# Ternary down product as two passes over divided rows, and the small inverse roots as a power on GpSimd

## The reference

```python
xn = layernorm(x)
x = x + L0_attn(xn) + L0_ffn(xn)        # layer 0
xn = layernorm(x)
x = x + L1_attn(xn) + L1_ffn(xn)        # layer 1: rotary attention; attention block and a top-2 mixture of 8 experts

def L0_ffn(x):                          # ternary weights, hidden width 1024
    gate, up = split(x @ ternary(w_gate_up).T)
    h = silu(gate) * up
    hn = h * rsqrt(mean(h * h) + eps)   # one factor per token, applied after the product in the kernel
    return hn @ ternary(w_proj).T       # the "down product"

def L0_attn(x):
    xn = rmsnorm(x)
    # q, k, v, gate, decay; a scan over time per (head, value) with a state S; group norm over 16 heads; silu gate; @ Wo
    x = x + gated @ Wo
    return x + swiglu(rmsnorm(x) * ln2) @ W2         # hidden width 704
```

## Time and profile before

| | |
|---|---|
| median of three runs | 671.49 us (668.30 to 672.75) |
| the profiled execution's own time | 671.92 us |
| its span in the trace | 670.1 us |
| mean granted TensorE clock | 0.938 of full |
| busy: PE, PE weight load | 570.6, 410.1 us |
| busy: DVE, ACT, POOL | 476.0, 309.0, 219.7 us |

### The profile page before, as it was taken

One profiled execution on the slowest core, in us unless ns is written; L12 is line 12 of the kernel. 1 busy time (PEld: TensorE's weight loads), 2 busy tenths in 40 slices (PEclk: granted clock), 3 DMA queues, 4 the chain that ended last, 5 costly groups with the idle time before them and its releaser, 6 DMA issues.

```text
span 670.1 us, 10996 instructions
## 1 busy us (share of the span) xinstructions
PE 570.6 (85%) x3694; PEld 410.1 (61%) x3694; DVE 476.0 (71%) x1054; ACT 309.0 (46%) x569; POOL 219.7 (33%) x226
## 2 busy tenths in 40 slices
PE   1777799889588999998999888988888799999990
PEld 1543467668367788883455545454444588888870
DVE  5789966797775477759787787778862477777753
ACT  2748322313322333551665635545537556666630
POOL 2667556546553533673200010010044012111210
PEclk9989889989698999995899999999989899999995
DMA  5221600000220000278353121200044891000005
GB/s 183 83 90 53 238 0 1 1 0 14 77 80 16 1 1 22 95 235 277 92 167 97 50 80 34 64 2 2 3 156 179 329 384 58 32 24 25 24 32 196
DMA packets 27404, 58.61 MB, mean 87 GB/s; under 512 B 4262, under 2 KB 19142, under 8 KB 24742
## 3 DMA queue, kind: packets, MB, share of 16 engines
q1 hardware_dynamic: 25094, 52.59, 24.2%
q0 software_dynamic: 1872, 5.13, 2.2%
q10 hardware_dynamic: 384, 0.20, 0.1%
HBM read 45.14 MB, written 15.51 MB: 90 GB/s over the span
## 4 chain that ended last, share of the span: by engine, by line
PE 40%; DVE 11%; ACT 3%; POOL 2%; issue 2%; DMA 1%; SPq 0%; ACTq 0%; POOLq 0%; DVEq 0%
PE bank L833 19%; DVE small L1826 5%; PE bank L1096 5%; PE bank L1073 4%; PE bank L827 4%; PE bank L1046 4%; PE bank L1048 1%; PE bank L1075 1%; ACT PTa L1381 1%; DMA yt<-results 1%; PE bank L1113 1%; POOL P3c L2254 1%; POOL rt L2194 1%; DVE XA L1855 1%; POOL P L2254 1%
## 5 line engine op out<-in xcount | busy, mean ns | idle before, releaser
L1826 DVE TENSOR_REDUCE small<-bank 128x1 f32<-128x256 f32 (+3 forms) x256 | 107.5, 483 | 7.5 <-PE bank L1048 6.6
L1046 PE MATMUL bank<-Ks,Qs 96*128 96x256 bf16 (+3 forms) x256 | 66.8, 328 | 8.7 <-DVE small L1826 7.1
L2088 DVE TENSOR_TENSOR wl<-wall,wh 128x1024 fp32r<-128x1024 f32 x46 | 56.2, 1222 | 22.0 <-ACT wh L1527 20.7
L1073 PE MATMUL bank<-Qs,Ks 99*128 99x512 bf16 (+3 forms) x256 | 59.4, 308 | 1.6 <-ACT PTa L1381 1.2
L1381 ACT ACTIVATE PTa<-bank 128x512 f32<-128x512 f32 (+1 forms) x96 | 43.5, 530 | 33.7 <-PE bank L1075 31.4
L1381 ACT ACTIVATE PTb<-bank 128x512 f32<-128x512 f32 (+1 forms) x96 | 43.8, 530 | 27.9 <-PE bank L1075 27.4
L1048 PE MATMUL bank<-maskb,identb 128*128 128x128 bf16 x256 | 55.4, 234 | 0.0
L1073 PEld LDWEIGHTS bank<-Qs,Ks 99*128 99x128 bf16 x256 | 25.5, 99 | 44.0 <-issue 24.0
L1330 ACT ACTIVATE sg<-bank 128x512 f32<-128x512 f32 (+1 forms) x28 | 16.7, 598 | 69.9 <-PE bank L833 69.9
L1527 ACT CAST wh<-wall 128x1024 fp32r x46 | 48.0, 1044 | 1.7 <-issue 0.5
L1075 PE MATMUL bank<-identb,maskb 128*128 128x128 bf16 x256 | 47.5, 223 | 0.0
(11 more groups left out here) (356 smaller groups left out, 1529.5 us busy)
## 6 DMA issues: line engine op xcount, KB each, us to landing
wall<-e_pack SPq DMA_DIRECT2D x8, 1536.0 KB, 8.7
Ks<-pieces SPq DMA_DIRECT2D x48, 128.0 KB, 2.6
Qs<-pieces SPq DMA_DIRECT2D x48, 128.0 KB, 2.7
stg<-w_pack SPq DMA_DIRECT2D x18, 256.0 KB, 2.8
pieces<-P SPq DMA_DIRECT2D x9, 512.0 KB, 5.1
wf<-t_pack SPq DMA_DIRECT2D x12, 256.0 KB, 2.7
sorted_rows<-blank_pack SPq DMA_DIRECT2D x1, 2967.0 KB, 14.3
yt<-results SPq DMA_DIRECT2D x8, 256.0 KB, 4.7
```

What stands on the lines that cost most here:

```text
L1046: nc.tensor.matmul(banks[b][:, o:o + w], Q[0:96, h, i * P:(i + 1) * P], K[0:96, h, 0:w], start=True, stop=False)
L1073: nc.tensor.matmul(banks[b][:, o:o + w], K[0:99, h, j * P:(j + 1) * P], Q[0:99, h, j * P:CH], start=True, stop=False)
L1826: last = nc.vector.tensor_reduce(mxv[:, i, h:h + 1], banks[b][:, o:o + w], AX.X, ALU.max, negate=True)
L2088: nc.vector.tensor_tensor(weight_part("l", i, half), wall[:, bass.ds(place + half * KC * EI, KC * EI)], weight_part("h", i, half).bitcast( ...
```

## The change

1. Down product. ACT casts hm to fh (fp32r), DVE makes fl = hm - fh (fp32r), and PE multiplies both with wpr as fp32r, two single passes in place of one fp32 product. `out` now waits for fl of its step. The item ("fl", s) is in the slot of `in`, one late on DVE, with no rank, so it stands behind the scan of that slot. On ACT the cast stands in front of the square.
2. Roots. All roots of 4 and 8 columns past the first norm are made by one POOL instruction, `inverse_roots`: small[:, 1] = small[:, 0] to the power -0.5, which waits for the DVE instruction that makes v (`variances_ready`); the users of the root wait for `inverse_roots`. A column of -0.5 is set at the start.
3. Order. In slots under 35 the DVE items that make v of `ss` and of ("rms", 0) come first in their slot; the users ("ssx", and ("rms", c, 1)) come last in theirs. The first norm (slots before 0) and the 64-column roots are as before.

```diff
+        m7, _ = plan([("fixed", [CH], F32), ("fh", [2, CH], F32R), ("fl", [2, CH], F32R)], o)
...
-            put(FF_SLOT[s], ("in", s), ("hm", s))
+            put(FF_SLOT[s], ("in", s), ("hm", s), ("fl", s))
...
-        put(22, ("ss", 0))
-        put(34, ("ss", 1))
+        put(22, ("ss", 0), ("ssx", 0))
+        put(34, ("ss", 1), ("ssx", 1))
...
+                if engine == "DVE" and slot < SW_AT and (op == "ss" or it == ("rms", 0, 0)):
+                    op = "first"
...
             def mlp_out(s, yb):
-                pe.wait_ge(*(hmr if kind == "ff" else alr).upto(s))
+                pe.wait_ge(*(flr if kind == "ff" else alr).upto(s))
...
-                        terms = [(hm[:, r, t * P:(t + 1) * P], L0["wpr"][:, m, :].bitcast(F32))]
+                        terms = [(part[:, s % 2, t * P:(t + 1) * P], L0["wpr"][:, m, :]) for part in (L0["fh"], L0["fl"])]
...
             def mlp_high(s):
+                    if s >= 2:
+                        act.wait_ge(*y.upto(s - 2))
+                    else:
+                        act.wait_ge(*t_put.upto(PIECES[-1]))
+                    nc.scalar.copy(L0["fh"][:, s % 2, :], hm[:, s % 3, :]).then_inc(*fhr.tick(s))
...
+            def mlp_low(s):
+                dve.wait_ge(*fhr.upto(s))
+                if s >= 2:
+                    dve.wait_ge(*y.upto(s - 2))
+                nc.vector.tensor_tensor(L0["fl"][:, s % 2, :], hm[:, s % 3, :], L0["fh"][:, s % 2, :].bitcast(F32), ALU.subtract)\
+                    .then_inc(*flr.tick(s))
...
+            def ff_squares(c):
+                dve.wait_ge(*mm.upto(("ss", c)))
+                nc.vector.tensor_scalar(small[:, 0, 0:TPC], banks[3][:, 0:TPC], 1.0 / 1024, EPS_F32, ALU.mult, ALU.add)\
+                    .then_inc(*var.tick(("ff", c)))
+                dve.wait_ge(*var.upto(("ff", c)))
...
             def ff_out(c):
-                rsqrt(r, v, TPC, 4)
+                dve.wait_ge(*inv.upto(("ff", c)))
...
-                    elif it[2] in (1, 2):
-                        rms_factors(it[2])
-                    else:
+                    elif it[2] == 1:
+                        rms_squares(("xm", c))
+                    elif it[2] == 3:
                         ln2_rows(c)
...
+            def inverse_roots(key, n):
+                pool.wait_ge(*var.upto(key))
+                nc.gpsimd.tensor_tensor(small[:, 1, 0:n], small[:, 0, 0:n], minus_half.broadcast_to([P, n]), ALU.pow).then_inc(*inv.tick(key))
...
+                elif op == "ss":
+                    inverse_roots(("ff", it[1]), TPC)
+                elif op == "rms" and it[2] == 0:
+                    inverse_roots(("rms", it[1]), TPC)
+                elif op == "xm" and it[2] == 1:
+                    inverse_roots(("xm", it[1]), TPC)
+                elif op == "ln" and it[2] == 0:
+                    inverse_roots(("norm", it[1]), 2 * TPC)
```

More of the change, by code:

```diff
@@ L170, in build @@
         ah_at = mlp_at + (2 + 3) * CH * 4
+        minus_half = small[:, 11, 63:64]
         QSX = at("QSX", [6, CH], F32, ah_at)
@@ L521, in build @@
         put(29, ("wo", 0, 1))
-        put(32, ("rms", 0, 0))
+        put(32, ("rms", 0, 0), ("rms", 0, 1))
         put(33, ("xat", 0, 0), ("xat", 0, 1))
@@ L541, in build @@
         put(SW_AT + SWO_AT[2], ("l1", 0, "xt", 0), ("l1", 0, "xt", 1))
-        LATE = {"PE": {}, "ACT": {"hm": 1}, "POOL": {"hm": 1, "read": 1},
-                "DVE": {"upd": 1, "scan": 1, "tern": 1, "hm": 1, "tr": 1, "proj": 1, "otok": 1, "wo": 1, "ss": 1, "got": 1, "xat": 1}}
+        LATE = {"PE": {}, "ACT": {"hm": 1}, "POOL": {"hm": 1, "read": 1, "ss": 1},
+                "DVE": {"upd": 1, "scan": 1, "tern": 1, "hm": 1, "fl": 1, "tr": 1, "proj": 1, "otok": 1, "wo": 1, "ss": 1, "ssx": 1, "got": 1, "xat": 1}}
         RANK = {"PE": ("rep", "in", "tern", "red", "out"), "ACT": ("in", "hm", "ternA"),
-                "POOL": ("read", "tern", "hm"), "DVE": ("tern0", "hm", "upd", "tern", "scan")}
+                "POOL": ("read", "tern", "hm"), "DVE": ("first", "tern0", "hm", "upd", "tern", "scan")}
         def order_of(engine):
@@ L1600, in norm_stats, with norm_squares @@
                     dve.wait_ge(*factors.upto(c))
+            def norm_squares(c):
+                v = small[:, 0, 0:2 * TPC]
+                stats(X, c)
+                tell(nc.vector.tensor_scalar(v[:, 0:TPC], mv[:, :, 1], EPS, None, ALU.add))
+                nc.vector.tensor_scalar(v[:, TPC:2 * TPC], mv[:, :, 1], 1.0 + EPS, EPS * EPS, ALU.mult, ALU.add)\
+                    .then_inc(*var.tick(("norm", c)))
             def norm_rows(layer, c):
+                if layer == 1:
+                    dve.wait_ge(*inv.upto(("norm", c)))
                 r1, r2 = small[:, 1, 0:TPC], small[:, 1, TPC:2 * TPC]
@@ L1732, in group_norm, with rms_squares @@
                     nc.vector.tensor_tensor(nat(L0["cen"]), nat(L0["cen"]), wide(rs_), ALU.mult).then_inc(*tok.tick(("got", c)))
[L1734 to L1741, removed]
-                else:
-                    newton(r, v, TPC, 4, 2)
+            def rms_squares(key):
+                v = small[:, 0, 0:TPC]
+                link(nc.vector.tensor_tensor(v, mv[:, :, 0], mv[:, :, 0], ALU.mult))
+                nc.vector.scalar_tensor_tensor(v, v, EPS, mv[:, :, 1], ALU.add, ALU.add).then_inc(*var.tick(key))
+                dve.wait_ge(*var.upto(key))
             def rms_scale(c, dst, key):
                 r = small[:, 1, 0:TPC]
+                dve.wait_ge(*inv.upto(("rms", c)))
                 for t in range(TPC):
@@ L1756, in ln2_rows @@
                 dve.wait_ge(s_route, 16)
+                dve.wait_ge(*inv.upto(("xm", c)))
                 for t in range(TPC):
@@ L2004, in _ @@
                 elif op == "rms":
-                    for pr in range(2):
-                        dve.wait_ge(*dproj.upto(("wo", it[1], pr)))
-                    rms_rows(it[1], L0["cen"], "xat")
+                    c = it[1]
+                    if it[2] == 0:
+                        for pr in range(2):
+                            dve.wait_ge(*dproj.upto(("wo", c, pr)))
+                        stats(XA, c)
+                        rms_squares(("rms", c))
+                    else:
+                        rms_scale(c, L0["cen"], "xat")
                 elif op == "swout":
@@ L2010, in _ @@
                 elif op == "ln":
-                    (norm_stats if it[2] == 0 else norm_rows)(1, it[1])
+                    norm_squares(it[1]) if it[2] == 0 else norm_rows(1, it[1])
                 elif op == "l1":
```

27 lines of the change are left out of this document (14 added, 13 removed).

## The result

Over 20 runs the changed kernel takes 666.47 us in the median (663.44 to 672.61), the kernel before 670.39 (667.87 to 673.29). The ratio is 0.9942, with a 95% interval of 0.9923 to 0.9962: 0.6% faster. The forecast was 666.9 with a range of 661.0 to 672.0.

A forecast was written before the change was run, and what follows sets the result against it. PE was taken to bound the feed-forward slots, DVE's chain the xm attention. Terms +0.2, 0, -0.5 and -4.3 gave -4.6: the span of 670.1 becomes 665.5, the time forecast 666.9 us, range 661.0 to 672.0.

The forecast's parts named there:

- What fl costs: Feed-forward slots: fl adds 0.60 us on DVE to hm, upd and scan, 3.05 us a slot together.
- The port makes it 3.2: Steady feed-forward slots: read, acc and fl take turns at the shared SBUF port, so a slot takes 3.2 us.
- fl(0) and hm(1): First feed-forward step: fl(0) waits behind a read until 92.1, so hm(1) moves from 90.27 to 92.0, 1.7 us late.
- The reduction of the group norm 2.2 earlier: Feed-forward slots: the group norm's reduction on DVE starts 2.2 us earlier than before.
- v to power 6 us, X rows 132.6, down product 134.4, DVE idle 2 to 3 in front of fl(10), hm(11) 144.0: End of the first batch: power's wait about 6 us, X rows and down product 1.8 earlier, hm(11) 1.8 later.
- Then PE's shorter products win back half: hm(15) is 1.4 late.: Last feed-forward slots: of hm(12)'s 3 us delay, PE's shorter products recover half, leaving hm(15) 1.4 us late.
- the second rival: Feed-forward slots: fl waits for fh in every slot, DVE's slot is 3.4 to 3.6 us, time 670.5; chance 0.12.
- POOL's queue takes another 0.5: End of the slots: POOL's queue of reads and low parts loses another 0.5 us to fl(15), ending at 176.7.
- The power's price 0.5, upper end 1.3: Each power instruction on POOL, on 4 or 8 columns: taken as 0.5 us, bounds 0.2 to 1.3.
- First power 5.5 us slow: Rival: only the first power, at the first batch's stall, is slow by about 5.5 us, time 672.4; chance 0.07.
- rms of the second batch 0, last norm -0.5: Second batch: no change at the rms before its cen, and the second layer norm's rows 0.5 us earlier.
- xm -4.3: Layer 1's attention, two xm norms: DVE's root leaves the chain, 2.15 us gained each, -4.3 for both.

The follow-up runs named there:

- fh_first: Changed kernel with ACT's order within a slot turned round, so fh and the square precede the next step's sg; 662.32 us, ratio 0.9868.
- both_moves: Changed kernel with fh ahead of sg on ACT, first batch's power ahead of read and sum, first rms' power ahead of the last low part; 659.55 us, ratio 0.9848.
- down_only: Kernel before with the down product's part alone (fh, fl, two fp32r passes), small roots still Newton rounds on DVE; 668.46 us, ratio 0.9994.
- xm_only: Kernel before with nothing changed but the power in the two xm norms; 665.46 us, ratio 0.9921.
- roots_only: Changed kernel with the old fp32 down product straight from hm; powers and their order stay; 666.34 us, ratio 0.9936.
- power_ahead: Changed kernel with only POOL reordered: first batch's power ahead of read and sum, first rms' power ahead of the last low part; 663.19 us, ratio 0.9889.
- power_twice: Changed kernel with every power done twice, one behind the other; 671.73 us, ratio 1.0010.
- short_acc: Changed kernel with POOL's sum of squares over 8 of 512 columns in all but a batch's first step; 667.07 us, one run.
- fp32_ahead: Changed kernel with the powers early on POOL, the old fp32 down product and ACT's order unchanged; 661.25 us, ratio 0.9861.
- lows_later: both_moves with five of the six low parts of w1 and w3 behind POOL's last reads and the first rms' power; 663.19 us, ratio 0.9870.

## Why the prediction was right, and where it was not

The mechanism in the attention was right. The total was right by compensation, and in part by luck: the terms below, with their measured sizes, add up to only 1.7 of the 3.9 us that were measured. 0.67 us of the +2.96 in the table had come before the first hm; 2.3 belong to the stage. By the steps of the prediction:

- *"What fl costs": DVE 3.05 us a slot.* Right, measured 3.04, with PE's sum just as long. *The port makes it 3.2*: wrong in steady slots. DVE's fl was in time and POOL's read paid, 1.66 instead of 1.29 us, which POOL had to spare. The wait itself is there: fl(6) starts at 112.43 beside a read that ends at 113.02 and lasts 1.14. The Trainium skill ("GPSIMD Engine Reference", 1. Specifications) says that such instructions contend; the trace agrees, 1.66 and 1.14 against 1.29 and 0.67. The rule was right, and yet it was no bound here.
- *fl(0) and hm(1).* hm(1) was forecast at 92.0 and came at 92.56, with the stage 0.67 late. But the reason was another: fl(0) had 1.14 us of idle time for ACT's cast, not for the read.
- *The reduction of the group norm 2.2 earlier.* It started at 119.79; before, at 122.24. Counted from the first hm that is 3.1 us earlier, 0.9 more than I had.
- *v to power 6 us, X rows 132.6, down product 134.4, DVE idle 2 to 3 in front of fl(10), hm(11) 144.0.* Measured 6.7, 133.20, 135.01, 2.73 and 144.56. Less the 0.67 us by which the stage began late, the three times hold within 0.2 us; from v to the end of the power it is 0.7 more than I had. It is luck that the times fit so well: the port's 0.16 us a slot did not come, and waits for fh at fl(0), fl(2), fl(6) and fl(7) that I hadn't counted there took their place.
- *"Then PE's shorter products win back half: hm(15) is 1.4 late."* This is the step that failed. hm(15) came at 162.87 instead of 160.5. 0.67 of that is the late start and 0.35 came before hm(12) (cen x small took 2.31 us beside a read, where it was the read that paid in the earlier trace rows); the other 1.3 is this step. From hm(12) to hm(15) I had 11.7 us, it was 13.03, and 13.32 before: almost nothing was won back, since fl(13) and fl(14) waited 1.26 and 0.65 for fh and fl(14) lasted 1.28. In fh_first and in both_moves the same stretch takes 11.66, what I had forecast. The waits for fh are the second rival, which I had at 0.12 for every slot. It bites in seven of 16. fh_first, which takes most of the waits away, shows their price: 4.2 us of the stage, 1.4 up to hm(10), 1.5 from there to hm(11) and 1.4 from hm(12) to hm(15).
- *POOL's queue takes another 0.5.* From hm(15) to the end of the last low part it was 15.71 us before and 16.15 after, +0.44: right.
- *The power's price 0.5, upper end 1.3.* Mis-sized: 1.02 us on 4 columns, and on 8 columns 1.65, outside my bounds. The two sizes give 0.158 us a column (worked out from them). It costs the 0.5 too much on every waited path.
- *First power 5.5 us slow.* Didn't happen: 1.04 for the first, 1.02 for the next ones. The 6 us that the Trainium skill ("GPSIMD Engine Reference", 2.1 Instruction dispatch) gives for the first call to a freshly loaded kernel do not show on this instruction.
- *rms of the second batch 0, last norm -0.5.* From the last XA tile to the end of cen it is 6.36 us before and 6.70 after, because cen beside qkv0's split takes 2.51 instead of 1.14: +0.3. From v to the end of the last XA rows it is 7.42 and 7.23: -0.2.
- *xm -4.3.* From the statistics to the rows 10.12 and 10.11 became 8.06 and 8.05: -4.1.

With the measured sizes the sum is +2.3 + 0.3 - 0.2 - 4.1 = -1.7, and 0.7 were lost before the slots. The profiled pair shows -4.8, so some 3.8 come from elsewhere, 2.8 up to the add in front of the experts and 0.9 at the very end. The 2.8 lie behind the second xm norm, where both kernels have the same program. There the granted clock differs, as the busy time by stretch shows (us, PE, weight load, DVE, ACT, POOL, clock, DMA; the same microseconds of both traces, and the changed kernel is up to 3.9 us further in its work there). The kernel before, then the changed kernel:

```profile
499.00:502.00 3.00, 3.00 (x21) 2.78 (x19) 0.12 (x1) 1.24 (x3) 0.00 (x0) 0.65 0.93 367
518.00:528.00 10.00, 6.91 (x58) 3.34 (x55) 3.45 (x7) 4.08 (x9) 0.00 (x0) 0.83 0.82 278
```

```profile
499.00:502.00 3.00, 1.55 (x16) 0.94 (x15) 1.29 (x5) 1.94 (x4) 0.00 (x0) 1.00 0.99 405
518.00:528.00 10.00, 7.92 (x68) 5.68 (x68) 4.34 (x9) 5.46 (x10) 0.00 (x0) 1.00 1.02 396
```

Where the kernel before stood at 0.65 and 0.83 the changed kernel had full clock. The same 32 products in either trace:

```profile
521.37 4.04 PE L1096 MATMUL bank<-PTb,Va 128*17 128x512 f32 x32 [0.80 <-ACT PTb L1381]
```

```profile
518.84 2.35 PE L1104 MATMUL bank<-PTb,Va 128*17 128x512 f32 x32 [0.80 <-ACT PTb L1394]
```

Is that the change's doing? From the statistics of the second xm norm to the add in front of the experts, less 2.06 us where the old root stands in it, it is 87.2 us before and 84.4 after. But down_only, with the old root, has 83.9, and fh_first and both_moves, with the powers, 87.6 and 88.6; xm_only, whose trace follows the one before within 0.3 us up to the first xm norm, has 84.0. Both lengths occur with either program, so I don't count these 2.8 us to the change; with one trace for each kernel, what decides between them isn't shown. That leaves the medians of 20 runs, which are 3.9 us apart (2.5 to 5.2 by the interval) where the sum of the terms is 1.7. xm_only, whose sum is 4.1, came out 4.9 below the kernel before. So 0.8 us or more of gain has no place in this account; that stays open. One place where it may lie is the stretch from the first rms' cen to the second's. At 24 to 28 us into it the granted clock is at 0.50 to 0.52 before, in xm_only, roots_only, power_ahead and in the changed kernel's trace, and the stretch takes 39.4 to 40.7 us. In down_only, fh_first, power_twice, short_acc and both_moves it is at full clock, and the stretch takes 36.3 to 37.6 (fp32_ahead lies between, at 0.69 and 38.1). If more executions of the changed kernel than of the kernel before take the short form, its median gains; one trace can't tell. The 0.67 us ahead of the slots stay out of it: over the twelve traces the first hm starts anywhere from 85.44 to 87.77.

## What to carry over

When an operation is split into parts on other engines, look at each part's place in the queue of its engine before pricing the part: here the cast takes 0.6 us and the power 1.0, and standing behind the next step's activation cost 4.2 us, behind a read and a sum and the last low part 4.4. A shorter bound engine gives its gain back only where nothing waits: the steady slots fell from 3.82 to 3.04 us, and the stage still became 2.3 longer, since nearly every other slot had a wait in it. And a total that fits isn't evidence for its terms: compare stage by stage, and test the stages.

## What was not expected of the hardware

The power on POOL costs 1.02 us for 128 x 4 and 1.65 for 128 x 8, while the sum of 128 x 8 in short_acc takes 0.2: it is the power that costs, and more for more columns. In the pairs looked at where DVE and POOL both work from SBUF, the one that starts later pays, whichever engine it is. Before, cen x small on DVE started 0.17 us ahead of a read, kept its 1.20, and the read took 2.17; after, the read starts 0.42 us ahead and cen takes 2.31. Against several instructions in a row the delay adds up: the rms' cen beside three low parts took 3.89 us in lows_later, 1.14 alone.

The granted clock of one and the same stretch differs from trace to trace, with the same work on PE. The last part before the second rms' cen, in the changed kernel and then in power_twice:

```profile
206.04:219.43 13.39, 13.36 (x74) 11.33 (x72) 5.47 (x15) 2.44 (x5) 5.23 (x6) 0.85 0.08 20
```

```profile
208.05:219.66 11.61, 10.49 (x69) 9.12 (x67) 5.19 (x15) 2.09 (x4) 5.93 (x7) 1.00 0.08 23
```

Both windows begin 26 us behind the first rms' cen and end with the second's. At 0.85 it takes 13.39 us, at the full clock 11.61, and that though power_twice has one more power in it. The two are different kernels, so whether the execution or what ran before decides the clock isn't shown. Two such places are about as much as the change itself.
